# One lent SBUF region, the first six message groups gathered beside the softmax, and the accumulator cleared on ScalarE

## What is computed

```python
h_e = jnp.einsum('nf,hfd->hnd', x, W_e)
h_r = jnp.einsum('nf,hfd->hnd', x, W_r)
...
score = s_src + s_dst + ... abs(diff) ... + ... hr_src * hr_dst ...   # one per edge and head
alpha = jax.nn.leaky_relu(score, negative_slope=ALPHA)
m = jax.ops.segment_max(alpha_t, src, num_segments=N)
ex = jnp.exp(alpha_t - m[src])
denom = jax.ops.segment_sum(ex, src, num_segments=N)[src]
att = ex / (denom + EPS)
msg = att[:, :, None] * jnp.transpose(h_e[:, dst], (1, 0, 2))
out = jax.ops.segment_sum(msg, src, num_segments=N)
...
x = x + gat(layernorm(x));  x = x + experts(layernorm(x))
```

## Time and profile before

| | us |
|---|---|
| median of 3 runs | 1518.27 (1517.32 to 1519.15) |
| the profiled execution, its time | 1517.85 |
| its span in the trace | 1516.1 |
| `score_edges` begins, ends | 226.8, 781.0 |
| last group's reduction ends on PE | 741.5 |
| softmax: last copy to `att` ends (ACT) | 770.2 |
| `sum_messages` begins | 781.0 |
| last add to `acc` ends (DVE) | 1172.8 |

### The profile page before, as it was taken

The page is one execution under the profiler, slowest core; times in us unless marked ns, Lnnn a source line. Parts: engine busy times, 40 slices in busy tenths (PEclk is TensorE's granted clock), DMA queues, the critical chain, the costliest instruction groups (busy, mean ns, idle before and its releaser), DMA issues. The chain is left out here.

```text
span 1516.1 us, 25712 instructions
## 1 busy us (share of the span) xinstructions
PE 1281.4 (85%) x6763; PEld 747.1 (49%) x6764; DVE 1207.1 (80%) x2409; ACT 1013.3 (67%) x2459; POOL 876.0 (58%) x953
## 2 busy tenths in 40 slices
PE   6999939999999999999539999999998056999940
PEld 2555525555555555555325555555554035777730
DVE  8998778999999999999748999999999953212217
ACT  5555417888989899898547898888886033555510
POOL 2100017777777777776647777777775803665520
PEclk9999969999999999999759999999999576999975
DMA  8111127888887887888569877777775093343439
GB/s 234 42 63 71 49 94 222 229 232 235 224 231 235 231 230 231 236 227 240 169 214 371 248 225 230 227 234 248 227 225 145 15 329 135 132 131 131 136 119 345
DMA packets 127712, 295.35 MB, mean 195 GB/s; under 512 B 29090, under 2 KB 45206, under 8 KB 127466
## 3 DMA queue, kind: packets, MB, share of 16 engines
q0 software_dynamic: 62880, 207.55, 46.6%
q1 hardware_dynamic: 62634, 85.29, 16.8%
q10 hardware_dynamic: 2080, 1.05, 0.3%
HBM read 247.91 MB, written 45.92 MB: 194 GB/s over the span
## 5 line engine op out<-in xcount | busy, mean ns | idle before, releaser
L1166 PE MATMUL m_ps<-msg,hot 128*128 128x512 f32 x672 | 369.5, 643 | 29.1 <-ACT msg L1108 28.9
L1085 POOL DMA_INDIRECT g<-he_d,target x288 | 293.4, 1019 | 94.1 <-issue 72.2
L927 PE MATMUL gs_ps<-room,hot_t 128*128 x1008 | 274.1, 381 | 10.3 <-DVE hot_t L787 8.7
L1002 ACT ACTIVATE uv<-ab,raw_a 128x512 f32<-128x512 f32 x336 | 273.7, 815 | 11.2
L768 POOL DMA_INDIRECT x_sb<-table_d,target x220 | 231.2, 1051 | 72.4 <-issue 51.2
L1000 ACT ACTIVATE ab<-d_ps 128x512 f32<-128x512 f32 x336 | 196.1, 584 | 74.9 <-PE d_ps L940 73.9
L798 DVE TENSOR_TENSOR uv<-uv,ab 128x512 f32<-128x512 f32 x336 | 229.3, 682 | 3.0 <-ACT uv L1002 2.8
L1136 DVE TENSOR_TENSOR room<-m_ps,room 128x512 f32 x336 | 229.8, 684 | 1.5 <-PE m_ps L1166 0.4
L1168 PEld LDWEIGHTS den_ps<-room,hot 128*128 128x128 f32 x672 | 129.2, 192 | 163.9 <-issue 163.9
L1129 DVE TENSOR_TENSOR msg<-g,room 128x384 f32<-128x384 f32 x336 | 184.4, 549 | 27.9 <-DMA g<-he_d,target 23.2
L1108 ACT ACTIVATE msg<-g,room 128x64 f32<-128x64 f32 x672 | 168.9, 334 | 56.3 <-DMA g<-he_d,target 52.9
(11 more groups left out here) (304 smaller groups left out, 2035.8 us busy)
## 6 DMA issues: line engine op xcount, KB each, us to landing
early_d<-early_rows SPq DMA_DIRECT2D x48, 256.0 KB, 3.1
g<-early_d SPq DMA_DIRECT2D x12, 1024.0 KB, 7.6
x_sb<-local_d SPq DMA_DIRECT2D x84, 128.0 KB, 4.2
w_sb<-in_L_ffn_W_dram SPq DMA_DIRECT2D x16, 512.0 KB, 8.0
pair_rows<-pairs_d SPq DMA_DIRECT2D x8, 1024.0 KB, 13.0
table_d<-row POOLq DMA_DIRECT2D x20, 260.0 KB, 2.6
he_d<-he SPq DMA_DIRECT2D x20, 256.0 KB, 2.0
xn_d<-xn SPq DMA_DIRECT2D x10, 512.0 KB, 4.9
```

The lines of the kernel that those rows point to most:

```text
L927: pe.matmul(gs_ps[:, use(n, t) % 3, :], h, hrs[:, bass.ds(blk, 1), piece, :].rearrange("p a f -> p (a f)"), start=(piece == 0), stop=(piec ...
L1002: act.activation(uv[:, j, c, :], ab[:, j, c, :], ACT.Identity, bias=raw[:, 0, c:c + 1], scale=raw[:, 1, c:c + 1]).then_inc(ur, 1)
L1085: pool.indirect_dma_start(g[:, r, t, :, :, :].rearrange("p c h d -> p (c h d)"), None, he_d, bass.IndirectOffsetOnAxis(ap=k["target"][:, q ...
L1166: pe.matmul(m_ps[:, i % BK, :], hot[:, r, t, :], msg[:, r, t, :, :, :].rearrange("p c h d -> p (c h d)"), start=True, stop=True).then_inc( ...
```

## The change

It has five parts.

- A tensor `rows` is held from the projection to the end of the messages. Projection puts its weights, `prod`, `xt` and `row` there, scoring puts `ab`, `uv` and `gd_more` there, and `sum_messages` its ring `g` of six groups. `hm` and `run` of the softmax move from `ab` to `extra`.
- The early groups are six instead of twelve: 9, 22, 35, 48, 61, 74. Their 24 tiles are gathered at the same 24 turns beside the scoring as the first 24 before. The 24 gathers and 24 writes behind the scoring go.
- POOL, once the last group of the scoring has been reduced (it waits for `dturned`, `extras` and `red`), gathers the 24 tiles of groups 0 to 5 straight into their places in `rows` (`msg_rows`). In `sum_messages` POOL starts with group 6.
- POOL's memset of `acc` goes. ACT clears it instead, with copies of `iota` scaled by zero: 14 of 20 blocks of 512 columns in one instruction behind the last score copy, then one block after each of the six exps.
- SP brings `x` back behind the load of group 9 instead of 7.

The rows below are POOL's program from the end of the scoring into the messages, first of before.

```diff
+CLEAR_FIRST = 14
...
-EARLY_EVERY, EARLY_ROOM = 7, 3
-EARLY = -(-G // EARLY_EVERY)
-BESIDE = GT * EARLY // 2
+AHEAD, EARLY_ROOM = 6, 3
+EARLY_GROUPS = tuple(range(9, G, 13))
+ROWS_ROOM = 2 * CH * LC * 2 + (RING - FLAT) * GT * TW
...
 (score_edges, SP)
-                for e in range(BESIDE, GT * EARLY):
-                    keep_early(e)
                 for j in range(EARLY_ROOM):
-                    sp.wait_ge(early_out[j], 16 * len(range(j, GT * EARLY, EARLY_ROOM)))
+                    sp.wait_ge(early_out[j], 16 * len(range(j, GT * len(EARLY_GROUPS), EARLY_ROOM)))
...
 (score_edges, POOL)
-                for e in range(BESIDE, BESIDE + GT * EARLY // 4):
-                    gather_early(e)
-                pool.wait_ge(gathered, GT * G)
-                pool.memset(k["acc"], 0.0).then_inc(cleared, 1)
-                for e in range(BESIDE + GT * EARLY // 4, GT * EARLY):
-                    gather_early(e)
-                pool.wait_ge(cleared, 1)
+                pool.wait_ge(dturned, CH * G)
+                pool.wait_ge(extras, G)
+                pool.wait_ge(red, G)
+                for n in range(AHEAD):
+                    q = message_tile(n)
+                    for t in range(GT):
+                        pool.indirect_dma_start(k["msg_rows"][:, n, t * F:(t + 1) * F], None, he_d,
+                                                bass.IndirectOffsetOnAxis(ap=k["target"][:, q + t:q + t + 1], axis=0)).then_inc(k["msg_rows_in"][n], 16)
...
 (score_edges, ACT, ahead of the loop over the six exps)
+                def clear(lo, hi):
+                    act.activation(k["acc"][:, lo * F:hi * F].rearrange("p (b q j) -> p b q j", q=CH, j=P),
+                                   bcast(bcast(k["iota"][:, :], 1, CH), 1, hi - lo), ACT.Copy, scale=0.0).then_inc(cleared, 1)
+
+                act.wait_ge(gathered, GT * G)
+                clear(0, CLEAR_FIRST)
...
+                    if CLEAR_FIRST + n < NB:
+                        clear(CLEAR_FIRST + n, CLEAR_FIRST + n + 1)
+                act.wait_ge(cleared, 1 + NB - CLEAR_FIRST)
...
 (sum_messages)
-        g = s.sb("g", [P, ROWS, GT, CH, 2, D])
+        g = k["msg_rows"].rearrange("p r (t c h d) -> p r t c h d", t=GT, c=CH, h=2)
...
-                for n in range(0, G, EARLY_EVERY):
+                for i, n in enumerate(EARLY_GROUPS):
...
-                    if n == EARLY_EVERY:
+                    if i == 0:
                         sp.dma_start(x_sb[:, 0:NB - 1, :], ...
...
-                for n in range(G):
+                for n in range(AHEAD, G):
                     if is_early(n):
                         continue
                     r, q = n % ROWS, first_tile(n)
-                    if n >= ROWS:
-                        pool.wait_ge(made, GT * (n - ROWS + 1))
-                        pool.wait_ge(made_act, GT * (n - ROWS + 1))
+                    pool.wait_ge(made, GT * (n - ROWS + 1))
+                    pool.wait_ge(made_act, GT * (n - ROWS + 1))
...
+            k["rows"] = e.sb("rows", [P, ROWS_ROOM])
+            k["msg_rows"] = k["rows"][:, 0:AHEAD * GT * F].rearrange("p (r w) -> p r w", r=AHEAD)
+            k["msg_rows_in"] = [sem(f"m_rows_in{r}") for r in range(AHEAD)]
```

More of the change, by code:

```diff
@@ L47 @@
 KEY_TURNS = (32, 34, 37, 39, 41)
-assert EROWS * EC == E and Q * P >= E + (NB - 1) * (P - 1) and STRIPS * TG == G and EROWS <= 96 and EC <= F
-EARLY_EVERY, EARLY_ROOM = 7, 3
-EARLY = -(-G // EARLY_EVERY)
-BESIDE = GT * EARLY // 2
+CLEAR_FIRST = 14
+assert EROWS * EC == E and Q * P >= E + (NB - 1) * (P - 1) and STRIPS * TG == G and NB - CLEAR_FIRST <= TG and EROWS <= 96 and EC <= F
+AHEAD, EARLY_ROOM = 6, 3
+EARLY_GROUPS = tuple(range(9, G, 13))
+ROWS_ROOM = 2 * CH * LC * 2 + (RING - FLAT) * GT * TW
 MSG_ORDER = [(TG - 1 - n // STRIPS, n % STRIPS) for n in range(G)]
@@ L65, in early_turn @@
     past = [m for m in range(EARLY_ROOM, n) if m % 10 in (0, 4, 8)]
-    now = n >= EARLY_ROOM and n % 10 in (0, 4, 8) and len(past) < BESIDE
+    now = n >= EARLY_ROOM and n % 10 in (0, 4, 8) and len(past) < GT * len(EARLY_GROUPS)
     return len(past) if now else None
@@ L133, in project_and_sort @@
         s = Space(nc, ctx)
-        w_e = s.sb("w_e", [P, CH, F])
-        w_r = s.sb("w_r", [P, CH, F])
+        part_of = lambda n: k["rows"][:, n * CH * F:(n + 1) * CH * F]
+        w_e = part_of(0).rearrange("p (c f) -> p c f", c=CH)
+        w_r = part_of(1).rearrange("p (c f) -> p c f", c=CH)
         a_all = s.sb("a_all", [P, HEADS, 4 * D])
-        prod = s.sb("prod", [P, CH, HEADS, D])
+        prod = part_of(2).rearrange("p (c h d) -> p c h d", c=CH, h=HEADS)
         lin = s.sb("lin", [P, CH, 2 * HEADS])
@@ L146, in project_and_sort @@
         xn = s.sb("xn", [P, 2, F])
-        xt = s.sb("xt", [P, XT, CH, P])
-        row = s.sb("row", [P, XB, TW])
+        xt = part_of(3).rearrange("p (r c n) -> p r c n", r=XT, c=CH)
+        row = k["rows"][:, 4 * CH * F:4 * CH * F + XB * TW].rearrange("p (r w) -> p r w", r=XB)
         he = s.sb("he", [P, 2, F])
@@ L687, in score_edges @@
         s = Space(nc, ctx)
-        gd_more = s.sb("gd_more", [P, RING - FLAT, GT, TW])
+        half = 2 * CH * LC
+        ab, uv = (k["rows"][:, n * half:(n + 1) * half].rearrange("p (r c j) -> p r c j", r=2, c=CH) for n in range(2))
+        gd_more = k["rows"][:, 2 * half:].rearrange("p (r t w) -> p r t w", t=GT, w=TW)
         rows_of = lambda n: k["gd"][:, n % RING, :, :] if n % RING < FLAT else gd_more[:, n % RING - FLAT, :, :]
@@ L698, in score_edges @@
         extra = s.sb("extra", [P, 2, GT, CH, 16, 2])
+        spare = extra[0:1, :, :, :, :, :].rearrange("p r t c s h -> p (r t c s h)")
+        hm = spare[:, 0:4 * P].rearrange("p (n c h s) -> p n c h s", n=4, c=CH, h=2)
+        run = spare[:, 4 * P:6 * P].rearrange("p (n c h s) -> p n c h s", n=2, c=CH, h=2)
         al = s.sb("al", [P, L])
@@ L1027, in sum_messages @@
 def sum_messages(nc, k, sem, x, he_d, early_d):
-    RING, ROWS, BK = 4, 6, 6
+    RING, ROWS, BK = 4, AHEAD, 6
     HV = 3
@@ L1043, in sum_messages @@
         made, made_act, offs = sem("m_made"), sem("m_made_act"), sem("m_off")
-        got = [sem(f"m_rows_in{r}") for r in range(ROWS)]
+        got = k["msg_rows_in"]
         xback, clear, den_done = sem("x_back"), sem("x_tail_then_den_clear"), sem("den_done")
@@ L1702, in kernel_body @@
     local_d = dram("local_d", [G, LC], BF16)
-    early_d = dram("early_d", [EARLY * GT * P, F], F32)
+    early_d = dram("early_d", [len(EARLY_GROUPS) * GT * P, F], F32)
     xn_d = dram("xn_d", [NB * P, F], F32)
```

27 lines of the change are left out of this document (10 added, 17 removed).

## The result

The changed kernel takes 1527.22 us (median of 4 runs, 1525.89 to 1530.23), the kernel before 1517.8 us in the same measurement (1516.42 to 1519.15). The ratio is 1.0062, 95% interval 1.0049 to 1.0075: slower by 9.4 us. The forecast was 1522.8, its range 1516.5 to 1527.5. Its profiled span is 1525.0 us against 1516.1.

The account below looks back on a forecast made before the run. The prediction took POOL's gather issue to bound the message block. A block start 1.2 us earlier and POOL's gathers 5.9 us later gave +4.7 us, 1522.5 on the profiled execution and 1522.8 as forecast, range 1516.5 to 1527.5.

Parts of the forecast that it names:

- the sum: Whole kernel: block start 1.2 us earlier, POOL's thirteenth message gather 5.9 us later relative to it, in all +4.7 us.
- the likeliest case: Whole kernel: slower by 3 to 7 us, a time of 1521.3 to 1525.3 us, chance 0.52.
- rival D: End of scoring: long drain, or gathers held by DVE's scans; +7 to +11 us, 1525 to 1529, chance 0.13.
- The end of the ahead-gathers: Between scoring and messages: POOL's 24 gathers start at 741.5 us, take 1.06 us each and end at 774.2.
- The rule on the DVE that blocks a DMA: Gathers beside the softmax: by the skill all 24 would take 0.95 us, ending at 771.5, the sum below 2.7 us smaller.
- The scoring block's drain: End of scoring on POOL: 5.4 us behind the last gather, so messages begin at about 779.9, 1.2 us earlier.
- Rival A: End of scoring: no drain paid behind gathers without pauses; block begins 9.1 us earlier, -3.2 us, 1515.0, chance 0.07.
- The clears on ACT: Softmax: the long clear takes 6.5 us and hides in ACT's slack, six short ones in its waits; cost nothing.
- The start of POOL in the messages: Message block: first gather 4.2 us behind ACT's first instruction, then a 2.2 us wait; thirteenth gather 5.9 us later.
- The end of the messages is POOL's beat: Message block: ends with POOL's first gather, 288 gathers at 1.324 us each, the last landing and last group's work.
- Rival B: Message block: DVE waits for transfers, not issues, so a six-group lead counts; some -11 us, 1507, chance 0.06.

Follow-up runs that it names:

- The seventh place: Changed kernel with group 6 given its own place in the message ring and ACT's `off` cut from four places to two: 1524.98 us, ratio 1.0033.
- the early groups from 15 on: Changed kernel with early groups 15, 27, ..., 75 instead of 9, 22, ..., 74: 1525.97 us, ratio 1.005.
- five groups ahead: Changed kernel gathering five groups ahead instead of six, so 20 gathers ahead and 292 in the messages: 1523.85 us, ratio 1.0031.
- ten early groups: Changed kernel with early groups 9, 16, ..., 72 instead of six, leaving 272 gathers in the messages: 1513.27 us, ratio 0.9963.

## Why the prediction was right, and what it left out

The direction and the mechanism in the message block were right; the sum, +4.7 us, was half of the measured 9.4, and one term of it was missing. That the range held is luck. The measured 1527.22 lies 0.3 us under its upper end and outside the likeliest case (1521.3 to 1525.3). It lies where rival D stood, with a chance of 0.13, and D's causes did not occur: the gathers ahead were short and the scoring block's drain was 5.1 us. The range reached up there for D's sake, and a drain that no rival had named filled the gap.

- *The end of the ahead-gathers.* Predicted start 741.5, end 774.2. Measured 743.89 and 774.68. The start came 2.4 late. PE's last product of the scoring ended at 745.1 (before 743.2); in the kernel with ACT's clears alone, whose scoring is that of the kernel before, it ended at 745.2. Over all the kernels here with 24 gathers beside the scoring it ended between 742.5 and 746.3. So this is the scoring's own spread, not a cost of the change. The gathers were shorter than the 1.06 us I chose: mean 0.991, for the bound of 0.95 that I had at the other end.
- *The rule on the DVE that blocks a DMA* (the Trainium skill, SBUF — State Buffer, the box): by the prediction's reading all 24 would take 0.95 us. 19 of the 24 took 0.94 to 0.99, five 1.14 or 1.15, all five between 756 and 768 us, in the midst of the softmax. The 0.95 is nearer than my mean. The prediction passed over a sentence of the same page, in the section "Who interferes with whom": a tensor_tensor with both inputs in SBUF contends with GpSimd's reads. The trace agrees with that sentence in the messages (the 62 longer gathers, shown above), and shows the same of another instruction in the softmax. Each of the five starts with 0.33 us left of DVE's scalar_tensor_tensor (the first at 756.44, while that ran from 756.02 to 756.76), whose inputs lie in SBUF, and lasts 0.82 beyond it; one of 0.99 starts with 0.17 left. The gather of 1.71 that the prediction held against the rule starts with 0.96 left of a scan. The mean of 0.991 saved 1.7 us against my term, which is most of what the late start cost.
- *The scoring block's drain.* Predicted 5.4 us behind the last gather, measured 5.1; the block began at 780.0 instead of 779.9. Rival A (not paid) and the long drain of rival D are out: 4.6 to 5.7 us in every kernel of this study.
- *The clears on ACT.* Predicted 6.5 us, measured 6.18; the first exp still waited 3.06 us for DVE, the others 1.56 and four times 1.07. Hidden, as said. That the memset leaves POOL's path is worth something only where POOL's early gathers stay behind the scoring: with this part alone 5.8 us by the medians (1519.3 to 1513.5) and 2.6 by the traces; with the region beside it 3.8 (1518.51 to 1514.7).
- *The start of POOL in the messages.* Predicted 4.2 us behind ACT's first instruction, measured 4.74; then a wait of 2.2 before group 10, measured 2.46, and a small one of 0.79 that I had not seen (group 7 waits for DVE's part of group 1, which was done about 10 us behind ACT's first instruction and not 9.4). The thirteenth gather came 23.0 behind, predicted 22.3. The seventh place and the early groups from 15 on each took one of the waits away and gave back 3.5 and 1.7 us at the last gather, counted from the block's start.
- *The end of the messages is POOL's beat.* Held everywhere: five groups ahead moved the last gather by -4.9 with four gathers more, ten early groups by -12.5 with 16 gathers fewer. Rival B is out: the beat stayed at 1.33 us (784.82 to 1166.35 for 287 gathers), and a lead of six groups bought nothing. DVE waited for no rows before 900 us and 28.6 us for them afterwards.
- *The step that failed* is the sum: it stopped at the last add and let everything behind it shift by as much; the end of the block was put at nothing, without a reason. The prediction looked at the drain of the block in front and at those of projection and experts, and not at the one at the end of `sum_messages`, whose own row stood in the trace. Its end there was 1.7 us behind POOL's last work, in the shade of DVE. In the changed kernel it is 8.6 us and closes the block: +5.4. With 1.3 us given back in the later blocks, -1.0 + 6.6 - 0.8 + 5.4 - 1.3 = +8.9 on the spans.
- *What makes that drain long* is shown in part. Chance, the memset and the region are out. It needs neither gathering ahead nor another number of gathers: with the ring where it had been and nothing ahead, another choice of early groups made it 6.5 us longer and the kernel 8.4 us slower by the medians of two sets (in the traces 7.6 to the start of the next block, 5.0 of them the drain's). The changed kernel has another choice too, which is enough to explain its drain; but all eight kernels that gather ahead have a long one, and none of them has the old choice, so whether gathering ahead would do it by itself isn't shown. By which rule the choice counts stays open; neither group 0 nor the last early group explains it alone.

## What to carry to other kernels

Work taken ahead of a block helps only if the queue that ends the block gets shorter or starts sooner; six groups lying ready with the same 288 gathers behind them helped nothing, while sixteen gathers fewer shortened the row of gathers by 19.3 us. The beat itself is not POOL's alone: a gather that starts inside a DVE instruction with both inputs in SBUF lasts until 0.82 us behind that instruction's end, some 20 us in all here (the estimate above). Where a full ring is handed over, its first refill waits for a consumer: leave one place empty. Count a block to its barrier and not to its last useful instruction, and read the end of every engine's drain against the end of its last work, because one that ends 1.3 us inside DVE's shade today can be the block's end after a change to the work in front of it.

## What was unexpected of the hardware

POOL's DRAIN behind a block with indirect DMAs goes on after POOL's last compute instruction, although the last gather was issued 40 to 42 us earlier and its rows have been used: 1.7 us in three kernels, 3.0 in a fourth, 7.3 to 9.2 in the others, the same to the ns in the changed kernel's two executions and to 6 ns in three kernels with one pattern. Its lengths differ by steps of 326.6 ns. Most message gathers take either 0.95 or about 1.28 us, which is 0.33 apart, but that length follows from how much of DVE's instruction is left when the gather starts; nothing here ties it to the drain's steps.

That relation is as exact: a gather's duration is what is left of DVE's instruction plus 0.82 us, to about 0.01, for the 62 longer message gathers of the changed kernel. One that starts inside DVE's scan lasts 0.75 beyond it (1.71 us with 0.96 left, in the kernel before).
